# VectorE empties the up bank right behind the norm, and o's low part is made between q's and k's

## The chip, the cores and the metric

The kernel runs on one core of one Trainium2 chip. The metric is the device time of one execution in microseconds (us). Before the change three runs gave 794.05, 796.18 and 797.39 us; the median is 796.18. One more execution was recorded by the hardware profiler; it took 795.6 us, and its span, on which all positions below are counted, is 793.8 us.

## The reference, cut to what matters

```python
x = L0_attn_x                                    # 1 x 4096 x 256, float32
x = x + attention(layernorm(x), w_qkv, w_out)    # 16 heads of 16, rope, phi = elu(.) + 1,
                                                 # causal linear attention: running sums of k*v and of k
x = x + experts(layernorm(x), Wg, Wu, Wd, Wr)    # 8 experts, 256 wide, all of them computed:
                                                 # h = silu(x @ Wg) * (x @ Wu); sum over experts of w * (h @ Wd)
return x
```

The routing weights `w` come from `sigmoid(x @ Wr / temperature)` with a zone test and a top-2 fallback. All is float32; the kernel reaches that precision by splitting each operand into a high and a low part and adding three products.

## The kernel before, in words

The 4096 tokens are cut into 32 tiles of 128 for attention, and into 8 blocks of 512 (four tiles) for the experts. A block has 16 units, two halves of each of eight experts. For one unit TensorE makes `gate(n)` and `up(n)` (six matmuls of 512 columns each), and `down(n)` (twelve of 256 columns). The order of work on each of the five engines is written out by hand; between engines there are semaphores. Each engine goes through its own list strictly in order.

From line 1115 on VectorE's list is a loop over steps `s = 8 to 35`. A step works on three things at once: tile `a = s` (its q, k, v), tile `c = s - 1` (its attention output, projection and second layernorm) and four units `n` to `n + 3` of the block that lies behind. Every fourth step the routing of one block is done as well (`route_...`, some thirty small VectorE operations); it is called a routing step below. Tiles 7 to 31 are `c` in the 25 steps 8 to 32; in six of these (9, 13, ..., 29) there is routing.

The operations that the change and the prediction touch, with their lines:

- `norm(c)`, line 895: VectorE divides the attention output by its denominator and writes `nat`. TensorE then transposes it (`o_T`, line 387).
- `h_up(n + 1)`, line 1064: VectorE multiplies the gate's silu in `work` by the up product in the PSUM bank `up`, which empties that bank. TensorE's next `up(n + 2)` waits for it, and so does ScalarE's `h_hi(n + 1)`, behind which GpSimd makes `h_lo(n + 1)`.
- `q_lo(a)` and `k_lo(a)`, lines 833 and 851: VectorE makes the low parts of q and k. Both wait for ScalarE's `q_hi` and `k_hi`. SyncE then issues the DMA transposes of q and then of k (lines 1284 and 1291), and TensorE's `scores(a)` wait for both.
- `o_lo(c)`, line 905: VectorE makes the low part of the transposed output, behind ScalarE's `o_hi(c)` (line 627). TensorE's projection `proj(c)` (line 390) waits for it.
- `x1_add(c)`, line 911: VectorE adds the projection to x.

In a step TensorE's list (line 499) is `gate(n)`, `up(n)`, `qkv(a)`, `gate(n + 1)`, `state(c)`, `av(c)`, `down(n - 2)`, `up(n + 1)`, `down(n - 1)`, `o_T(c)`, `gate(n + 2)`, `proj(c)`, `up(n + 2)`, `gate(n + 3)`, `down(n)`, `scores(a)`, `x2_T(c)`, `down(n + 1)`, `up(n + 3)`. ScalarE's, around the place of the change: `exp(a)`, `silu(n + 1)`, `q_hi(a)`, `k_hi(a)`, `h_hi(n)`, `v1(a)`, `o_hi(c)`, `h_hi(n + 1)`, `silu(n + 2)`.

Of the kernel before, what the change touches and what calls it, by code (L numbers as in the profile page):

```python
# [45 lines left out]
def bcast(ap, axis, n):  # L46

    ap = ap.unsqueeze(axis)
    shape = list(ap.shape)
    shape[axis] = n  # L50
    return ap.broadcast_to(shape)
# [16 lines left out]
def build(nc, x, xT, w_qkv, w_out, Wg, Wu, Wd, Wr, temperature, tab, out):  # L68
# [8 lines left out]
    with ctx:  # L77
# [113 lines left out]
        def routed(b, step):  # L191

            return len(ROUTE) * b + ROUTE.index(step) + 1
# [17 lines left out]
        def qk_bank(g):  # L211

            return U if g < NT and g % 2 else R0
# [25 lines left out]
        def live(g):  # L239
            return 0 <= g < NTL  # L240
# [5 lines left out]
        def live_unit(n):  # L246
            return 0 <= n < UNITS * NB
# [469 lines left out]
        def vector_program(v):  # L717
# [58 lines left out]
            def x_lo(g):  # L776
                if not live(g):
                    return
                w.wait_ge(s_xhi, g + 1)
                v.tensor_tensor(xo[1][:, g % 2, :, :], xr[:, g % 2, :, :], xo[0][:, g % 2, :, :].bitcast(F32),  # L780
                                ALU.subtract).then_inc(s_xlo, 1)

            def bn(g):
                if not live(g):
                    return
                w.wait_ge(s_mv, g)
                w.wait_ge(xa_in[g % 4], 16 * (g // 4 + 1))
                v.bn_stats(bst[:, :], xa[:, g % NXA, :]).then_inc(s_bn, 1)

            def mean_var(g):  # L790
                if not live(g):
                    return
                w.wait_ge(s_ve, g)
                v.memset(idle[:, 0:1], 0.0)
                w.wait_ge(s_bn, g + 1)
                v.bn_aggr(mv[:, :], bst[:, :]).then_inc(s_mv, 1)
# [36 lines left out]
            def q_lo(g):  # L833
                if not live(g):
                    return
                w.wait_ge(s_qhi, g + 1)
                w.wait_ge(s_khi, g + 1)
                v.tensor_tensor(q_st[:, :, 2:4, :], bcast(qk_bank(g)[:, 0:D].rearrange("p (h d) -> p h d", d=HD), 2, 2),
                                q_st[:, :, 0:2, :], ALU.subtract).then_inc(s_qlo, 1)

            def mask(g, r):
                if not live(g):
                    return
                w.wait_ge(s_mask, 1)
                w.wait_ge(s_alo, am_free(g, r))
                w.wait_ge(s_qk, 2 * g + r // 2 + 1)
                v.tensor_tensor(am_place(g, r).rearrange("p (h n) -> p h n", h=4),  # L847
                                score_bank(g, r)[:, :].rearrange("p (h n) -> p h n", h=4), bcast(cmask[:, :], 1, 4),
                                ALU.mult).then_inc(s_amask, 1)

            def k_lo(g):
                if not live(g):
                    return
                k_s = k_st[:, g % 2, :, :, :]
                w.wait_ge(s_qhi, g + 1)
                w.wait_ge(s_khi, g + 1)
                v.tensor_tensor(k_s[:, :, 1::2, :], bcast(qk_bank(g)[:, D:].rearrange("p (h d) -> p h d", d=HD), 2, 2),
                                k_s[:, :, 0::2, :], ALU.subtract).then_inc(s_klo, 1)
# [36 lines left out]
            def norm(g):  # L895
                if not live(g):
                    return
                w.wait_ge(s_colmean, 2)
                w.wait_ge(s_x2T, g)
                w.wait_ge(s_rec, g + 1)  # L900
                v.scalar_tensor_tensor(out=nat[:, :].rearrange("p (h d) -> p h d", d=HD), in0=osb[:, :, 0:HD],
                                       scalar=1.0 / ASCALE, in1=bcast(rec[:, :], 2, HD), op0=ALU.mult,
                                       op1=ALU.mult).then_inc(s_norm, 1)

            def o_lo(g):
                if not live(g):
                    return
                w.wait_ge(s_ohi, g + 1)
                v.tensor_tensor(ox[1][:, :, :], oT, ox[0][:, :, :].bitcast(F32), ALU.subtract).then_inc(s_olo, 1)
# [47 lines left out]
            def route_sum(b):  # L957
                if not 0 <= b < NB:
                    return
                w.wait_ge(s_logit, b + 1)  # L960
                v.tensor_reduce(R["s2"], logits, AX.X, ALU.add).then_inc(s_route, 1)
# [32 lines left out]
            def route_first(b):  # L994
                if not 0 <= b < NB:
                    return
                w.wait_ge(s_route, routed(b, "eq"))
                v.scalar_tensor_tensor(out=R["c"], in0=R["eq"], scalar=99.0, in1=io, op0=ALU.mult,
                                       op1=ALU.add).then_inc(s_route, 1)
                w.wait_ge(s_route, routed(b, "w0"))  # L1000
                v.tensor_reduce(Q["ws"], R["w0"], AX.X, ALU.add).then_inc(s_route, 1)
                w.wait_ge(s_route, routed(b, "c"))
                v.tensor_reduce(Q["ix"], R["c"], AX.X, ALU.min).then_inc(s_route, 1)
                w.wait_ge(s_route, routed(b, "ws"))
                v.tensor_scalar(Q["no"], Q["ws"], 1e-8, None, ALU.is_lt).then_inc(s_route, 1)

            def route_second(b):
                if not 0 <= b < NB:
                    return
                w.wait_ge(s_route, routed(b, "ix"))  # L1010
                v.tensor_tensor(R["s1"], io, bcast(Q["ix"], 2, E), ALU.is_equal).then_inc(s_route, 1)
                w.wait_ge(s_route, routed(b, "s1"))
                v.scalar_tensor_tensor(out=R["nd"], in0=R["s1"], scalar=9.0, in1=R["dist"], op0=ALU.mult,
                                       op1=ALU.add).then_inc(s_route, 1)
                w.wait_ge(s_route, routed(b, "nd"))
                v.tensor_reduce(Q["m2"], R["nd"], AX.X, ALU.min).then_inc(s_route, 1)
                w.wait_ge(s_fb, b + 1)
                v.tensor_tensor(R["fw"], R["fb"], bcast(Q["no"], 2, E), ALU.mult).then_inc(s_route, 1)
# [45 lines left out]
            def h_up(n):  # L1064
                if not live_unit(n):
                    return
                w.wait_ge(s_g, n + 1)
                w.wait_ge(s_up, n + 1)
                v.tensor_tensor(hb[:, n % 2, :], hb[:, n % 2, :], U[:, :], ALU.mult).then_inc(s_h, 1)  # L1069
# [5 lines left out]
            def acc(n, t):  # L1075

                if not live_unit(n):
                    return
                b, e_ = n // UNITS, n % UNITS // KI
                xs = xa[:, (NT * b + t) % NXA, :]  # L1080
                w.wait_ge(*((s_last, t + 1) if n == LAST + 2 else (s_down, n // KI * KI + KI)))
                w.wait_ge(s_route, routed(b, "wo"))
                w.wait_ge(s_x2n, NT * b + t + 1)
                w.wait_ge(s_acc, NT * (n // KI) + t - 3)
                v.scalar_tensor_tensor(out=xs, in0=y_bank(n, t),  # L1085
                                       scalar=wo[:, b % 2, t, e_:e_ + 1], in1=xs, op0=ALU.mult, op1=ALU.add).then_inc(s_acc, 1)
# [28 lines left out]
            for s in range(8, STEPS):  # L1115
                a, c, n = s, s - 1, NT * (s - LAG)
                router = (s - LAG) // NT if (s - LAG) % NT == 0 else -1
                mask(c, 2); acc(n - 4, 0); bn(a + 1); mask(c, 3); route_sum(router)
                mean_var(a + 1); x_lo(a + 1); acc(n - 4, 1); acc(n - 4, 2); acc(n - 4, 3); h_up(n)
                var_eps(a + 1); route_zone(router); route_nearest(router); cos(a); st_add(c); rope(a); o_sum(c, 0)  # L1120
                o_sum(c, 1); den_max(c); phi(a); route_weight(router); den_rec(c); 
                route_first(router); norm(c); route_second(router); q_lo(a); k_lo(a); o_lo(c); h_up(n + 1)
                route_tie(router); x1_add(c); acc(n - 2, 0); bn2(c); route_ix2(router); acc(n - 2, 1)
                mean_var2(c); acc(n - 2, 2); route_s2(router); var_eps2(c); acc(n - 2, 3)
                h_up(n + 2); route_both(router); ln2(c); mask(a, 0); x2_lo(c); mask(a, 1); route_out(router)
                h_up(n + 3)

            n = LAST
# [240 lines left out]
```

## Time and profile before

| | |
|---|---|
| median of three runs | 796.18 us (794.05 to 797.39) |
| the profiled execution, its span | 795.6 us, 793.8 us |
| TensorE matmul busy | 772.2 us, 97% |
| TensorE weight load busy | 668.2 us, 84% |
| VectorE busy | 607.7 us, 77% |
| GpSimd busy | 481.9 us, 61% |
| ScalarE busy | 466.3 us, 59% |
| chain that ended last | TensorE 86%, VectorE 6%, GpSimd, ScalarE, DMA and issue 2% each |

Times of rows are microseconds from the start of the span. A matmul's end in the trace is modelled, and matmuls are pipelined, so the starts are what one compares: from the start of one group to the start of the next is what the group costs. An operation of VectorE or ScalarE also overlaps the next by some 0.1 us.

### The profile page before, as it was taken

The numbers are of one execution on the slowest core, as the hardware profiler recorded it, in microseconds if no ns is written. First come the engines' busy times: TensorE is split into PE (matmuls) and PEld (weight loads), VectorE is DVE, ScalarE is ACT, GpSimd is POOL, SyncE is SP. The second block draws the span as 40 slices with busy tenths as digits, with TensorE's granted clock in tenths as the row PEclk, the third lists the DMA queues.
The fourth block names the chain that finished last, engine by engine and source line by source line (L and its number), as shares of the span: only waits on it lengthen the run. The fifth ranks groups of instructions, "written<-read, shape, count | busy, mean of one in ns | idle before, by whom it ended". The sixth has DMA issues, their size and how long they took to land.

```text
span 793.8 us, 18445 instructions
## 1 busy us (share of the span) xinstructions
PE 772.2 (97%) x6864; PEld 668.2 (84%) x6864; DVE 607.7 (77%) x1565; ACT 466.3 (59%) x886; POOL 481.9 (61%) x537
## 2 busy tenths in 40 slices
PE   9778899999999999999999999999999999999998
PEld 8666788888888888888888888888888888888887
DVE  7898877879777797778877797788877788756343
ACT  5665776656656656565666566657656666634222
POOL 4886667756566576655666656566676655653322
PEclk9999999999999999999999999999999999999999
DMA  6635331122211031222201221120111121100000
GB/s 171 147 81 111 79 68 47 41 43 68 42 40 29 17 68 41 41 44 65 41 15 31 43 67 42 41 43 19 51 42 41 40 54 28 28 2 27 1 1 26
DMA packets 97320, 38.28 MB, mean 48 GB/s; under 512 B 74192, under 2 KB 96976, under 8 KB 97232
## 3 DMA queue, kind: packets, MB, share of 16 engines
q1 hardware_dynamic: 90704, 30.83, 18.0%
q10 hardware_dynamic: 6528, 6.29, 2.7%
q8 instruction: 54, 0.88, 0.5%
q14 instruction: 34, 0.28, 0.1%
HBM read 16.13 MB, written 4.19 MB: 26 GB/s over the span
## 4 chain that ended last, share of the span: by engine, by line
PE 86%; DVE 6%; POOL 2%; ACT 2%; DMA 2%; issue 2%; SPq 0%; ACTq 0%; DVEq 0%; POOLq 0%
PE y L478 21%; PE up L444 21%; PE gate L444 21%; PE front L304 5%; PE front L305 3%; PE back L356 3%; PE back L400 2%; PE up L375 2%; PE up L412 1%; PE front L327 1%; DMA qT<-q_st 1%; PE back L344 1%; PE front L425 1%; PE back L327 1%; PE y L275 1%
## 5 line engine op out<-in xcount | busy, mean ns | idle before, releaser
L1230 POOL TENSOR_TENSOR h_lo<-work,h_hi 128x512 fp32r<-128x512 f32 x126 | 163.3, 1296 | 63.8 <-ACT h_hi L683 63.0
L1201 POOL TENSOR_TENSOR a_lo<-am,a_hi 128x512 f16<-128x512 f32 x120 | 142.2, 1186 | 52.1 <-ACT a_hi L610 49.6
L478 PE MATMUL y<-wd_hi,h_hi 128*128 128x256 f32 x504 | 145.9, 289 | 0.0
L478 PE MATMUL y<-wd_lo,h_hi 128*128 128x256 f32 x504 | 140.6, 279 | 0.0
L478 PE MATMUL y<-wd_hi,h_lo 128*128 128x256 f32 x504 | 140.4, 278 | 0.0
L1069 DVE TENSOR_TENSOR work<-work,up 128x512 f32<-128x512 f32 x128 | 86.9, 679 | 62.9 <-PE up L444 62.8
L683 ACT ACTIVATE h_hi<-work 128x512 fp32r<-128x512 f32 x126 | 79.3, 629 | 60.6 <-DVE work L1069 33.7
L1085 DVE SCALAR_TENSOR_TENSOR xa<-y,wo,xa 128x256 f32<-128x256 f32 x252 | 111.5, 470 | 2.0 <-PE y L478 2.0
L610 ACT ACTIVATE a_hi<-am 128x512 f16<-128x512 f32 x120 | 74.7, 625 | 41.9 <-DVE am L847 38.3
L478 PEld LDWEIGHTS y<-wd_hi,h_hi 128*128 128x128 f32 x504 | 94.7, 188 | 4.2 <-issue 0.2
L478 PEld LDWEIGHTS y<-wd_lo,h_hi 128*128 128x128 f32 x504 | 94.9, 188 | 2.7
L478 PEld LDWEIGHTS y<-wd_hi,h_lo 128*128 128x128 f32 x504 | 95.2, 189 | 0.0
L675 ACT ACTIVATE work<-gate 128x512 f32<-128x512 f32 x128 | 75.8, 592 | 32.5 <-PE gate L444 18.7
L444 PE MATMUL gate<-x_hi,wg_hi 128*128 128x512 f32 x256 | 82.6, 404 | 0.4 <-ACT work L675 0.4
L1189 POOL TENSOR_TENSOR vs<-vs,vx 128x256 f32<-128x256 f32 x32 | 21.5, 673 | 98.7 <-ACT vx L597 98.7
L444 PE MATMUL up<-x_hi,wu_hi 128*128 128x512 f32 x256 | 81.0, 398 | 0.1
L444 PE MATMUL gate<-x_lo,wg_hi 128*128 128x512 f32 x256 | 80.1, 394 | 0.0
L444 PE MATMUL gate<-x_hi,wg_lo 128*128 128x512 f32 x256 | 79.9, 394 | 0.0
L444 PE MATMUL up<-x_lo,wu_hi 128*128 128x512 f32 x256 | 79.6, 392 | 0.0
L444 PE MATMUL up<-x_hi,wu_lo 128*128 128x512 f32 x256 | 79.5, 392 | 0.0
L1180 POOL TENSOR_TENSOR rop<-qk,tabs 128x256 f32<-128x256 f32 x64 | 46.1, 738 | 30.9 <-ACT qk L555 30.9
L444 PEld LDWEIGHTS gate<-x_hi,wg_lo 128*128 128x128 f32 x256 | 48.3, 189 | 11.0
(227 smaller groups left out, 1773.8 us busy)
## 6 DMA issues: line engine op xcount, KB each, us to landing
xr<-xT SPq DMA_DIRECT2D x32, 128.0 KB, 2.5
xa<-x SPq DMA_DIRECT2D x32, 128.0 KB, 2.5
out<-xa SPq DMA_DIRECT2D x32, 128.0 KB, 1.7
xa<-Wg ACTq DMA_DIRECT2D x8, 256.0 KB, 2.7
work<-Wd ACTq DMA_DIRECT2D x8, 256.0 KB, 3.3
work<-Wu ACTq DMA_DIRECT2D x8, 256.0 KB, 2.9
work<-w_qkv SPq DMA_DIRECT2D x2, 384.0 KB, 3.6
kT<-k_st SPq DMA_TRANSPOSE x32, 3.1
```

The costliest lines, as they stand in the source:

```text
L304: pe.matmul(qk_bank(g)[:, :], lhs, wqkv_p[wi][:, k, 0:2 * D], start=first, stop=last)
L305: m = pe.matmul(R1[:, 0:D], lhs, wqkv_p[wi][:, k, 2 * D:], start=first, stop=last)
L444: m = pe.matmul(ps, weights[wi][:, e_, k, m_ * P:(m_ + 1) * P], x2[xi][:, b % 2, k, :], start=(n == 0), stop=(n == 3 * KD - 1))
L478: m = pe.matmul(y_bank(n, t), h_at(hi, n)[:, t * P:(t + 1) * P], wd_p[wi][:, u // KI, u % KI, :], start=(n % KI == 0 and (t % 2 == 0 or n ...
L610: act.activation(a_p[0][:, heads(r), :], am_place(g, r).rearrange("p (h n) -> p h n", h=4), ACT.Copy).then_inc(s_ahi, 1)
L675: act.activation(hb[:, n % 2, :], G[:, :], ACT.Silu).then_inc(s_g, 1)
L683: act.activation(h_at(0, n), hb[:, n % 2, :], ACT.Copy).then_inc(s_hhi, 1)
L1069: v.tensor_tensor(hb[:, n % 2, :], hb[:, n % 2, :], U[:, :], ALU.mult).then_inc(s_h, 1)
L1085: v.scalar_tensor_tensor(out=xs, in0=y_bank(n, t), scalar=wo[:, b % 2, t, e_:e_ + 1], in1=xs, op0=ALU.mult, op1=ALU.add).then_inc(s_acc, 1)
L1180: pool.tensor_tensor(r2_h[:, :, half, :], qk_h[:, :, 1 - half, :], bcast(tabs[:, g // NT % 2, g % NT, at:at + HALF], 1, 2 * H), ALU.mult). ...
L1201: pool.tensor_tensor(a_p[1][:, heads(r), :], am_place(g, r).rearrange("p (h n) -> p h n", h=4), a_p[0][:, heads(r), :], ALU.subtract).then ...
L1230: pool.tensor_tensor(h_at(1, n), hb[:, n % 2, :], h_at(0, n).bitcast(F32), ALU.subtract).then_inc(s_hlo, 1)
```

## The change

Two edits in one line of VectorE's loop. `h_up(n + 1)` goes from behind `o_lo(c)` to right behind `norm(c)`, ahead of the routing's `route_second` and of `q_lo(a)`. And `o_lo(c)` changes places with `k_lo(a)`. Nothing is added or taken away, and the lists of the four other engines stay as they are.

```diff
@@ -1119,7 +1119,7 @@
                 o_sum(c, 1); den_max(c); phi(a); route_weight(router); den_rec(c); 
-                route_first(router); norm(c); route_second(router); q_lo(a); k_lo(a); o_lo(c); h_up(n + 1)
+                route_first(router); norm(c); h_up(n + 1); route_second(router); q_lo(a); o_lo(c); k_lo(a)
                 route_tie(router); x1_add(c); acc(n - 2, 0); bn2(c); route_ix2(router); acc(n - 2, 1)
```

VectorE's instructions in a step without routing, before (-) and now (+). L901 is `norm`, L838 `q_lo`, L857 `k_lo`, L909 `o_lo`, L1069 `h_up`, L916 `x1_add`; behind each stand the semaphores that it waits for:

```order
 L901 SCALAR_TENSOR_TENSOR nat<-osb,rec 128x256 [waits rec,x2_T]
-L838 TENSOR_TENSOR q_st<-front,q_st 128x16x32 [waits k_hi,q_hi]
-L857 TENSOR_TENSOR k_st<-front,k_st 128x32x16
-L909 TENSOR_TENSOR ox_lo<-back,ox_hi 128x256 [waits o_hi]
-L1069 TENSOR_TENSOR work<-work,up 128x512 [waits up,g]
+L1069 TENSOR_TENSOR work<-work,up 128x512 [waits up,g]
+L838 TENSOR_TENSOR q_st<-front,q_st 128x16x32 [waits k_hi,q_hi]
+L909 TENSOR_TENSOR ox_lo<-back,ox_hi 128x256 [waits o_hi]
+L857 TENSOR_TENSOR k_st<-front,k_st 128x32x16
 L916 TENSOR_TENSOR xa<-back,xa 128x256 [waits proj]
```

`h_up` moved up past three operations, and `o_lo` past one; `x1_add` has the same four in front of it.

The same in a routing step, where L1011 to L1018 are the four operations of `route_second` (one of them, L1016, stands between the two pieces of the difference):

```order
 L901 SCALAR_TENSOR_TENSOR nat<-osb,rec 128x256 [waits rec,x2_T]
+L1069 TENSOR_TENSOR work<-work,up 128x512 [waits up,g]
 L1011 TENSOR_TENSOR router<-iota,q_ix 128x32 [waits router_step]
 L1013 SCALAR_TENSOR_TENSOR router<-router 128x32 [waits router_step]
...
 L1018 TENSOR_TENSOR router<-router,q_no 128x32 [waits fb]
 L838 TENSOR_TENSOR q_st<-front,q_st 128x16x32 [waits k_hi,q_hi]
-L857 TENSOR_TENSOR k_st<-front,k_st 128x32x16
-L909 TENSOR_TENSOR ox_lo<-back,ox_hi 128x256 [waits o_hi]
-L1069 TENSOR_TENSOR work<-work,up 128x512 [waits up,g]
+L909 TENSOR_TENSOR ox_lo<-back,ox_hi 128x256 [waits o_hi]
+L857 TENSOR_TENSOR k_st<-front,k_st 128x32x16
```

Here `h_up` also moved past `route_second`.

## Rows read from the trace of the kernel before

**Rows 1.** The page, part 1: busy time, share of the span, instructions.

```profile
PE 772.2 (97%) x6864; PEld 668.2 (84%) x6864; DVE 607.7 (77%) x1565; ACT 466.3 (59%) x886; POOL 481.9 (61%) x537
```

**Rows 2.** 400 to 500 us: busy PE, PEld, DVE, ACT, POOL (instructions); granted clock; DMA share, GB/s.

```profile
400.00:500.00 100.00, 100.00 (x891) 86.25 (x890) 80.23 (x207) 62.48 (x119) 64.61 (x72) 1.00 0.17 39
```

**Rows 3.** Waits, 200 to 700 us: total, times, longest.

```profile
PEld back L400 <- DVE ox_lo L909: 4.8, 22, 0.2
PE front L327 <- DMA kT<-k_st: 0.6, 1, 0.6
```

**Rows 4.** Timeline of TensorE's matmuls, step without routing: start, duration.

```profile
412.03 0.62 PE L444 MATMUL up<-x_lo,wu_hi 128*128 128x512 f32 x2
...
415.03 0.62 PE L444 MATMUL gate<-x_lo,wg_hi 128*128 128x512 f32 x2
415.50 0.47 PE L400 MATMUL back<-wout_hi,ox_hi 128*128 128x256 f32 x2
416.27 0.62 PE L444 MATMUL up<-x_hi,wu_hi 128*128 128x512 f32 x2
```

**Rows 5.** The same in a routing step.

```profile
278.55 0.62 PE L444 MATMUL gate<-x_lo,wg_hi 128*128 128x512 f32 x2
279.01 0.40 PE L400 MATMUL back<-wout_hi,ox_hi 128*128 128x256 f32 x2
279.71 0.62 PE L444 MATMUL up<-x_hi,wu_hi 128*128 128x512 f32 x2
```

**Rows 6.** Timeline of TensorE's weight loads, step without routing, then with.

```profile
415.46 0.30 PEld L400 LDWEIGHTS back<-wout_hi,ox_hi 128*128 128x128 f32 x2 [0.23 <-DVE ox_lo L909]
...
278.91 0.30 PEld L400 LDWEIGHTS back<-wout_hi,ox_hi 128*128 128x128 f32 x2 [0.17 <-DVE ox_lo L909]
```

**Rows 7.** Timeline of VectorE, step without routing.

```profile
412.12 0.42 DVE L901 SCALAR_TENSOR_TENSOR nat<-osb,rec 128x256 f32<-128x256 f32 x1
413.78 0.69 DVE L838 TENSOR_TENSOR q_st<-front,q_st 128x512 f16<-128x512 f32 x1 [1.24 <-ACT k_st L586]
414.39 0.68 DVE L857 TENSOR_TENSOR k_st<-front,k_st 128x512 f16<-128x512 f32 x1
414.99 0.41 DVE L909 TENSOR_TENSOR ox_lo<-back,ox_hi 128x256 fp32r<-128x256 f32 x1
415.32 0.67 DVE L1069 TENSOR_TENSOR work<-work,up 128x512 f32<-128x512 f32 x1
```

**Rows 8.** Timeline of ScalarE, the same step.

```profile
412.11 0.60 ACT L675 ACTIVATE work<-gate 128x512 f32<-128x512 f32 x1
413.08 0.60 ACT L586 ACTIVATE k_st<-front 128x512 f16<-128x512 f32 x1
414.39 0.39 ACT L632 ACTIVATE ox_hi<-back 128x256 fp32r<-128x256 f32 x1
```

**Rows 9.** Timeline of VectorE and ScalarE, routing step.

```profile
275.91 0.42 DVE L901 SCALAR_TENSOR_TENSOR nat<-osb,rec 128x256 f32<-128x256 f32 x1
277.23 0.69 DVE L838 TENSOR_TENSOR q_st<-front,q_st 128x512 f16<-128x512 f32 x1 [0.25 <-ACT k_st L586]
278.44 0.41 DVE L909 TENSOR_TENSOR ox_lo<-back,ox_hi 128x256 fp32r<-128x256 f32 x1
...
277.87 0.39 ACT L632 ACTIVATE ox_hi<-back 128x256 fp32r<-128x256 f32 x1
```

**Rows 10.** Timeline of SyncE's queue: the transposes of q and k.

```profile
414.50 1.24 SPq L1289 DMA_TRANSPOSE qT<-q_st  x1
415.84 1.27 SPq L1296 DMA_TRANSPOSE kT<-k_st  x1
...
279.28 1.28 SPq L1296 DMA_TRANSPOSE kT<-k_st  x1
```

**Rows 11.** The tile kT, 180 to 740 us: how long its transposes take to land.

```profile
DMA to landing us min/median/max: 3.1/3.1/5.3
```

**Rows 12.** Timeline of TensorE: the scores of the step of [rows 4].

```profile
420.53 0.40 PE L327 MATMUL front<-qT,kT 64*128 64x128 f16 x8
```

## The prediction

> **What bounds the kernel now.** I read the page first: TensorE's matmuls are busy 97% of the span, VectorE 77% [rows 1]. Then the table of busy time by stretch: between 400 and 500 us TensorE is busy for the whole 100.00 us at a granted clock of 1.00 (the 2.4 GHz level), VectorE for 80.23 [rows 2]. So in the loop only what TensorE waits for costs anything. The table of waits from 200 to 700 us shows what that is: the weight load of the projection (line 400) waited for `o_lo` in all 22 steps, 4.8 us together, and the scores waited once for k's transpose, 0.6 us [rows 3]. A waiting weight load isn't yet a lost matmul, so I went to the timeline. In a step without routing the projection starts at 415.50 and `up` behind it at 416.27: 0.77 us for six matmuls [rows 4]. In a routing step the same six take 279.01 to 279.71, 0.70 [rows 5]. The gate in front of both paces the same: its last pair starts 0.47 and 0.46 before the projection. The loss is 0.07, and its cause shows in the weight loads: 415.46 in the one, after 0.23 of waiting, 278.91 in the other, after 0.17 [rows 6]. Seen from the start of the gate's last pair that is 0.43 behind and 0.36 behind. A load 0.36 behind costs nothing that I can see; one 0.43 behind costs 0.07, since the second matmul's load is then late too.
>
> The 25 steps of tiles 7 to 31 hold six routing steps, and in the last one no `q_lo` stands ahead of `o_lo`. That leaves 18 steps with this pattern (I read 0.75 to 0.79 in them). All that VectorE's order can give back here is 18 x 0.07 = 1.3 us. Every other distance from group to group repeats to some 0.05 us (but for two or three late DMAs) whether VectorE is early or late, so I take it as TensorE's own pace.
>
> **The change part by part.** Nothing is added, so the sum is of what moves.
>
> `h_up` behind the norm, step without routing. The norm starts at 412.12 and the next operation, `q_lo`, at 413.78, with 1.24 idle in front, waiting for `k_hi` [rows 7]. `h_up` needs the silu, which ends at 412.11 + 0.60 = 412.71 [rows 8], and `up(n + 1)`, whose last pair of matmuls runs from 412.03 to 412.65 [rows 4]. A wait released by ScalarE takes 0.10 here (`k_hi` ends 413.08 + 0.60 = 413.68, `q_lo` starts 413.78), so `h_up` runs 412.81 to 413.48 with the 0.67 of its row [rows 7]. It fits into the idle time with 0.3 to spare, and `q_lo` stays at 413.78. Cost: nothing. If that cover went, every 0.1 by which `h_up` starts after 413.1 would be 0.1 on `q_lo`.
>
> `o_lo` ahead of `k_lo`. `o_lo` needs `o_hi`, which ends at 414.39 + 0.39 = 414.78 [rows 8]; it stands behind `q_lo`, whose successor started 0.61 after it, at 414.39. The later of the two decides: 414.78 + 0.10 = 414.88, against 414.99 now [rows 7]. So `o_lo` comes 0.11 earlier, not the 0.60 of the operation that it passes. The projection's weight load then starts at 415.46 - 0.11 = 415.35, which is 0.32 behind the gate's last pair, ahead of the 0.36 of the routing step that costs nothing. Gain: the whole 0.07, in 18 steps, -1.3 us. Bounds: 0 (the load remains late) and -1.4 (18 x 0.08, with the start of the projection itself).
>
> `k_lo` last of the three. It starts 0.33 behind `o_lo` (the distance from `o_lo` to its successor, 415.32 - 414.99 [rows 7]): 415.21, end 415.89, against 415.07 now. But SyncE isn't ready for it sooner: the transpose of q holds the queue from 414.50 to 415.74 and that of k is issued at 415.84 [rows 10]. So k's transpose goes from 415.84 to about 415.93, 0.09 later. It lands 3.1 later [rows 11], near 419.0, and the scores start at 420.53 [rows 12], 1.5 later. Cost: nothing. The loads of x behind it on the queue move by the same 0.09, for tiles two and more steps ahead. `x1_add`, next on VectorE, needs the projection, which ends near 416.3 (`up` starts behind it at 416.27 [rows 4]); `k_lo` has ended by then.
>
> The routing step has less room. `q_lo` starts 0.25 after the wait for `k_hi` began, at 277.23 [rows 9]. `h_up` now stands in front of `route_second`, and takes 0.60 from start to start as `k_lo` does (414.39 to 414.99 [rows 7]), so `q_lo` moves by 0.60 - 0.25 = 0.35, to 277.58, and lets its successor in at 278.19. `o_hi` ends at 277.87 + 0.39 = 278.26, so `o_lo` starts at 278.36, against 278.44 [rows 9]: no loss, 0.08 to the good, 0.17 between its two conditions. `k_lo` follows at 278.69 and ends at 279.37. SyncE gets q's transpose 0.35 later and k's at 279.28 + 0.35 = 279.63 [rows 10]; it lands near 282.7. The scores come some 5 us behind the projection (415.50 to 420.53 in [rows 4, 12]), so near 284.0: 1.3 of room. Cost of six such steps: 0; bounds 0 and, if `q_lo` held `o_lo` up by the full 0.35, 6 x 0.35 = +2.1.
>
> What `h_up` feeds. The bank `up` is free 2.5 us sooner, but the table of waits has no row of `up` waiting for it: `up(n + 2)` follows the projection at once. `h_hi(n + 1)` can follow `o_hi` at once, and `h_lo(n + 1)` comes some tenths sooner; its reader, `down(n + 1)`, runs behind the scores, after 420.53 [rows 12]. Gain: 0, since TensorE's list has other work there. Bounds 0 and -0.5.
>
> Sum: -1.3 + 0 + 0 = -1.3 us. Against the profiled execution, whose time is 795.6 (span 793.8 and 1.8 around it), that is 794.3. That execution lies 0.6 below the median of 796.18, so for the median I predict 796.2 - 1.3 = 794.9.
>
> **A rule against this sum.** Rows 2 show TensorE's matmuls at 100.00 of 100 us and the weight loads at 86.25. The Trainium skill (Perfetto Trace Analysis, Identifying the Most-Contended Engine) says that matmul busy time is a poor measure of how near TensorE is to its limit, and that the busy share of LDWEIGHTS is a good one. By that rule 13.75% of the loop would be room, and an earlier `h_up` could win more than my rows let me count. It is the last rival below.
>
> **The rivals.**
>
> 1. The wait is only handed on. `o_lo` is released by `o_hi`, 0.11 earlier than now; if the true release is nearer 0.2 than 0.10, the weight load stays late and nothing moves. For it: the gain hangs on 0.11 us. Against: the routing step shows how little is needed. Time: 796.2.
>
> 2. Slower: k's transpose becomes what the scores wait for. It goes out 0.09 later in ordinary steps and 0.35 later in routing steps. Once it took 5.3 us to land instead of 3.1 [rows 11], and TensorE then stood for 0.6 [rows 3]. If its new place, or the loads of x beside it, made that the rule, each of 25 steps would lose 5.3 - 3.1 - 1.5 + 0.1 = 0.8, so +20 us: 815 (with the 1.3 won, still over 814). It decides once landing takes more than 4.5. Against: TensorE waited for it once in the 22 steps of [rows 3], and it is a shift of 0.09 on a queue that is otherwise the same.
>
> 3. Slower by little: in routing steps `q_lo` holds `o_lo` up. It starts to cost when `q_lo` is over 0.17 later than I think. Price 0.35 x 6 = +2.1, less 1.3: 797.0.
>
> 4. TensorE has room. If the pace of the matmuls hid waits for VectorE, then freeing the bank 2.5 us sooner would give back up to the 0.67 of `h_up` in each of 25 steps: 17 us, 779. Against it: the same groups take the same time in routing steps, where VectorE works later, and in the others; a hidden wait would differ.
>
> **How the numbers follow.** Forecast 0.64, rival 1 0.20, rival 3 0.07, rival 2 0.04, rival 4 0.03, and 0.02 for what I haven't seen. The likeliest time is 794.9. The runs of before spread from 794.05 to 797.39 around their median, so a median carries some 1 to 1.5 us of its own; with the forecast (-1.4 to -1.2) and rivals 1 and 3 (0 to +0.8) the range is 793.0 to 797.4, and rivals 2 and 4 are left out of it. A measurement of this kernel can't tell less than about 0.5% (4 us) from no change. Forecast and rivals 1 and 3 all lie inside that, 0.91 together. Faster by more than that: rival 4 and a share of the unseen, 0.04. Slower: rival 2 and the rest, 0.05.
>
> **What would show it.** In the changed kernel's profile: `h_up` starting within 0.2 of the silu's end, and the idle time before `q_lo` down from 1.24 to about 0.6 or less in ordinary steps, and none in routing steps; `o_lo` 0.1 earlier against the norm; the projection's six matmuls at 0.70 in all steps, and the wait of its weight loads down from 4.8 us to about 2.5; `k_lo`'s end just at the moment its transpose is issued; the scores with no new wait for a DMA. The forecast is wrong if the projection still takes 0.77, if the scores or `o_T` show waits in most steps, or if a step without routing gets shorter by more than 0.1 us.

## The result, and the profile after

The changed kernel takes 800.77 us (median of 6 runs, 799.44 to 801.62) against 795.66 for the one before (6 runs): a ratio of 1.0061, 95% interval 1.0045 to 1.0078. It is slower by 5.1 us, where I had forecast 1.3 faster, a median between 793.0 and 797.4, and given "slower" one chance in twenty.

The ordinary steps (those without routing) did what was predicted; the routing steps lost over four times as much as these won. The timeline of TensorE shows both: the first matmul of `qkv` (L304) marks a step. Before the change, a routing step and then an ordinary one:

```profile
267.74 0.40 PE L304 MATMUL front<-wqkv_hi,xo_hi 128*128 128x512 f32 x1
...
290.31 0.39 PE L304 MATMUL front<-wqkv_hi,xo_hi 128*128 128x512 f32 x1
...
312.84 0.39 PE L304 MATMUL front<-wqkv_hi,xo_hi 128*128 128x512 f32 x1
```

After it, the same two:

```profile
269.39 0.40 PE L304 MATMUL front<-wqkv_hi,xo_hi 128*128 128x512 f32 x1
...
292.99 0.39 PE L304 MATMUL front<-wqkv_hi,xo_hi 128*128 128x512 f32 x1
...
315.43 0.39 PE L304 MATMUL front<-wqkv_hi,xo_hi 128*128 128x512 f32 x1
```

The routing step went from 22.57 to 23.60 us, +1.03; the ordinary one from 22.53 to 22.44, -0.09. The other steps repeat this within some hundredths, but for a few with a late DMA in either kernel, so 6 x 1.03 - 18 x 0.08 = +4.7 of the 5.1 us.

The ordinary step, VectorE's timeline after, answers to [rows 7]:

```profile
416.18 0.69 DVE L1069 TENSOR_TENSOR work<-work,up 128x512 f32<-128x512 f32 x1 [0.22 <-ACT work L675]
417.20 0.69 DVE L838 TENSOR_TENSOR q_st<-front,q_st 128x512 f16<-128x512 f32 x1 [0.33 <-ACT k_st L586]
418.22 0.42 DVE L909 TENSOR_TENSOR ox_lo<-back,ox_hi 128x256 fp32r<-128x256 f32 x1 [0.33 <-ACT ox_hi L632]
418.56 0.68 DVE L857 TENSOR_TENSOR k_st<-front,k_st 128x512 f16<-128x512 f32 x1
419.80 0.42 DVE L916 TENSOR_TENSOR xa<-back,xa 128x256 f32<-128x256 f32 x1 [0.56 <-PE back L400]
```

The norm started at 415.53. `q_lo` starts 1.67 behind it, as before (1.66), `o_lo` 2.69 behind instead of 2.87, and the projection's six matmuls take 0.69 to 0.72 us in every step. The row of `PEld back L400` waiting for `ox_lo` [rows 3] is gone from the table of waits. In its place stand three new rows on `down` (L478), from 200 to 700 us ("issue" is time in which the engine waited for nothing that the profile shows):

```profile
PEld y L478 <- issue: 3.7, 5, 0.7
PE y L478 <- DVE xa L1085: 2.8, 10, 0.3
PEld y L478 <- DVE xa L1085: 2.1, 5, 0.4
```

Five and ten times: once and twice in each routing step of the stretch. TensorE's timeline in one of them shows the price. The last pair of the gate starts at 283.64 and `down` 0.96 later, where it was 0.45 before, and halfway through `down` another 0.39 goes (the matmuls of 256 columns otherwise start 0.11 to 0.12 apart). That is 0.9 of the 1.03. After:

```profile
283.64 0.62 PE L444 MATMUL gate<-x_lo,wg_hi 128*128 128x512 f32 x2
284.60 0.36 PE L478 MATMUL y<-wd_hi,h_hi 128*128 128x256 f32 x1 [0.34 <-DVE xa L1085]
...
285.26 0.28 PE L478 MATMUL y<-wd_hi,h_lo 128*128 128x256 f32 x1
285.76 0.38 PE L478 MATMUL y<-wd_hi,h_hi 128*128 128x256 f32 x1 [0.22 <-DVE xa L1085]
```

Before:

```profile
282.00 0.62 PE L444 MATMUL gate<-x_lo,wg_hi 128*128 128x512 f32 x2
282.45 0.28 PE L478 MATMUL y<-wd_hi,h_hi 128*128 128x256 f32 x1
```

`down(n)` writes PSUM (the memory that matmuls write to) where VectorE's four `acc(n - 2, .)` (L1085) must first have read out the earlier `down`; each adds its part to `xa`, weighted. They stand behind `x1_add` in VectorE's list. Why they are late is in VectorE's own rows. After:

```profile
280.88 0.78 DVE L1024 TENSOR_TENSOR router<-router,q_m 128x32 f32<-128x32 f32 x1
281.70 1.22 DVE L1026 SCALAR_TENSOR_TENSOR router<-router,iota 128x32 f32<-128x32 f32 x1
282.84 0.41 DVE L916 TENSOR_TENSOR xa<-back,xa 128x256 f32<-128x256 f32 x1
```

Before:

```profile
279.37 0.65 DVE L1024 TENSOR_TENSOR router<-router,q_m 128x32 f32<-128x32 f32 x1
280.05 0.19 DVE L1026 SCALAR_TENSOR_TENSOR router<-router,iota 128x32 f32<-128x32 f32 x1
280.16 0.42 DVE L916 TENSOR_TENSOR xa<-back,xa 128x256 f32<-128x256 f32 x1
```

L1024 and L1026 are `route_tie`; both read two inputs in SBUF, the on-chip memory that the engines share. L1026 is the same instruction on 128x32 elements, and took 1.22 us instead of 0.19. Counted from the norm (277.57 and 275.91), it starts at 4.13 and 4.14, but `x1_add` behind it starts at 5.27 instead of 4.25: 1.02 later, and so does each `acc`, within 0.01. GpSimd's timeline says what else was going on. After:

```profile
280.33 2.54 POOL L1230 TENSOR_TENSOR h_lo<-work,h_hi 128x512 fp32r<-128x512 f32 x2
```

Before:

```profile
278.67 1.29 POOL L1230 TENSOR_TENSOR h_lo<-work,h_hi 128x512 fp32r<-128x512 f32 x1
280.32 1.29 POOL L1230 TENSOR_TENSOR h_lo<-work,h_hi 128x512 fp32r<-128x512 f32 x1 [0.35 <-ACT h_hi L683]
```

Before, GpSimd stood still for 0.35 us between `h_lo(n)` and `h_lo(n + 1)`, waiting for `h_hi(n + 1)`, and L1026 ran in just that gap (280.05 to 280.24). Since `h_up(n + 1)` is early, `h_hi(n + 1)` is early, and the two `h_lo` run back to back until 282.87; L1026 ends at 282.92. My theory (the port theory below) was that VectorE and GpSimd share a way into SBUF, so that VectorE's operation can't read beside GpSimd's and waits inside its own busy time. In ordinary steps the two `h_lo` now run back to back too (418.64, 2.55 us), but no operation with both inputs in SBUF stands there. The rivals were that VectorE's order by itself, or one of its own semaphores, makes the step late.

### The profile page after: what moved, and what is told of

Its sections match the earlier page's. It is cut to its first block, busy times and chain, and to the rows that moved or that the text cites. A ratio compares the mean times of both kernels' runs of the same rounds, so it can differ in the third digit from the quotient of the medians.

```text
span 799.5 us, 18445 instructions
## 1 busy us (share of the span) xinstructions
PE 771.5 (96%) x6864; PEld 667.7 (84%) x6864; DVE 618.4 (77%) x1565; ACT 466.0 (58%) x886; POOL 480.4 (60%) x537
## 4 chain that ended last, share of the span: by engine, by line
PE 76%; DVE 10%; ACT 5%; issue 4%; DMA 2%; POOL 2%; SPq 0%; ACTq 0%; DVEq 0%; POOLq 0%
PE up L444 19%; PE gate L444 19%; PE y L478 18%; PE front L304 5%; PE front L305 3%; PE up L375 2%; PE back L356 2%; PE back L400 2%; DVE xa L1085 1%; PE up L412 1%; DMA qT<-q_st 1%; PE front L327 1%; DMA kT<-k_st 1%; ACT L675 1%; DVE k_st L857 1%
## 5 line engine op out<-in xcount | busy, mean ns | idle before, releaser
L478 PE MATMUL y<-wd_hi,h_hi 128*128 128x256 f32 x504 | 146.9, 291 | 3.4 <-DVE xa L1085 3.4
L478 PE MATMUL y<-wd_lo,h_hi 128*128 128x256 f32 x504 | 140.6, 279 | 0.0
L478 PE MATMUL y<-wd_hi,h_lo 128*128 128x256 f32 x504 | 140.4, 279 | 0.0
L1069 DVE TENSOR_TENSOR work<-work,up 128x512 f32<-128x512 f32 x128 | 87.2, 682 | 67.0 <-PE up L444 63.2
L1085 DVE SCALAR_TENSOR_TENSOR xa<-y,wo,xa 128x256 f32<-128x256 f32 x252 | 111.5, 470 | 2.0 <-PE y L478 2.0
L478 PEld LDWEIGHTS y<-wd_hi,h_hi 128*128 128x128 f32 x504 | 94.7, 188 | 10.9 <-issue 4.4
L478 PEld LDWEIGHTS y<-wd_lo,h_hi 128*128 128x128 f32 x504 | 94.9, 188 | 2.4
L478 PEld LDWEIGHTS y<-wd_hi,h_lo 128*128 128x128 f32 x504 | 95.2, 189 | 0.0
```

The source lines that it names most:

```text
L478: m = pe.matmul(y_bank(n, t), h_at(hi, n)[:, t * P:(t + 1) * P], wd_p[wi][:, u // KI, u % KI, :], start=(n % KI == 0 and (t % 2 == 0 or n ...
L1085: v.scalar_tensor_tensor(out=xs, in0=y_bank(n, t), scalar=wo[:, b % 2, t, e_:e_ + 1], in1=xs, op0=ALU.mult, op1=ALU.add).then_inc(s_acc, 1)
```

## The experiments

Each is an edit of the changed kernel; the differences are shortened to the calls that matter. Each ratio is against runs of the kernel before on the same chip.

**The second edit alone.**

```diff
-norm(c); h_up(n + 1); route_second(router); q_lo(a); o_lo(c); k_lo(a)
+norm(c); route_second(router); q_lo(a); o_lo(c); k_lo(a); h_up(n + 1)
```

> The second edit alone: o_lo ahead of k_lo, h_up back behind them in all steps. Theory (port): VectorE's route_tie operations have both inputs in SBUF, and GpSimd's h_lo holds them up while it runs; in the changed kernel h_lo(n+1) follows h_lo(n) without the gap of 0.35 us that was there before, and L1026 takes 1.22 instead of 0.19. With h_up back, that gap returns in routing steps and L1026 takes 0.19 again, so nothing is lost there. But in ordinary steps h_up now ends about 0.5 us later than before (o_lo waits for o_hi with VectorE idle, then k_lo, then h_up), up(n+2) waits some 0.4 for it, 18 steps: 795.7 - 1.3 + 7 = about 802, all of the loss in ordinary steps. Rival (order): the routing step is late because o_lo, k_lo stand otherwise, whatever GpSimd does; then the routing steps stay 1.05 longer here.

Measured: 803.14, ratio 1.0100 (1.0083 to 1.0117). The size was right, and so was its place in the ordinary steps: `up` waits for `h_up`, in the waits from 200 to 700 us

```profile
PEld up L444 <- DVE work L1069: 7.1, 22, 0.3
```

L1026 takes 0.19, and a routing step 22.88 us, not the 23.6 that the rival (the order of `o_lo` and `k_lo` by itself) asks for. I had missed that routing steps also lose some 0.3, since `h_up` is late there too. So the two edits belong together: `o_lo` waits for `o_hi`, and without `h_up` ahead of it VectorE idles and then makes `h_up` late.

**The first edit alone.**

```diff
-route_second(router); q_lo(a); o_lo(c); k_lo(a)
+route_second(router); q_lo(a); k_lo(a); o_lo(c)
```

> The first edit alone: h_up right behind the norm, o_lo behind k_lo as before. Port theory: the collision is there as in the changed kernel (L1026 1.2 us, six routing steps 1.05 longer: +6.3), and the 0.07 in 18 ordinary steps is not won: 795.7 + 6.3 = 802.0, or 1.3 slower than the changed kernel. Rival (the swap is at fault): no loss in routing steps, 795.7.

Measured: 801.79, ratio 1.0081 (1.0067 to 1.0096). As the port theory said. Groups of VectorE, 200 to 700 us (count, busy, mean ns, idle before):

```profile
L1026 DVE SCALAR_TENSOR_TENSOR router<-router,iota 128x32 f32<-128x32 f32 x5 | 6.1, 1222 | 0.2
L1024 DVE TENSOR_TENSOR router<-router,q_m 128x32 f32<-128x32 f32 x5 | 4.8, 959 | 0.0
```

Routing steps take 23.60 us as in the changed kernel, ordinary ones 22.53 as before. The loss comes with `h_up`'s move, not with the swap.

**`route_tie` later, in routing steps.**

```diff
-route_tie(router); x1_add(c); acc(n - 2, 0); bn2(c); route_ix2(router); acc(n - 2, 1)
-mean_var2(c); acc(n - 2, 2); route_s2(router); var_eps2(c); acc(n - 2, 3)
+x1_add(c); acc(n - 2, 0); bn2(c); acc(n - 2, 1); route_tie(router)
+mean_var2(c); acc(n - 2, 2); route_ix2(router); var_eps2(c); acc(n - 2, 3); route_s2(router)
```

> The changed kernel with route_tie moved behind acc(n-2, 1), and route_ix2 and route_s2 each one place on, in routing steps; ordinary steps are unchanged. Port theory: VectorE's two-input operations no longer stand in front of x1_add while GpSimd runs h_lo(n) and h_lo(n+1); x1_add starts 4.0 to 4.3 us behind the norm instead of 5.28, down(n) waits little: 794.4, at most 796. Rival (VectorE has simply too much to do in a routing step since the change): the same work is only reordered ahead of acc(n-2, 3), and down(n) still waits about 1 us in its second half: 800.

Measured: 794.53, ratio 0.999 (0.998 to 1.000), with the two `h_lo` still back to back (278.27, 2.55 us). The same operations, now behind them, take

```profile
280.94 0.18 DVE L1024 TENSOR_TENSOR router<-router,q_m 128x32 f32<-128x32 f32 x1
281.15 0.19 DVE L1026 SCALAR_TENSOR_TENSOR router<-router,iota 128x32 f32<-128x32 f32 x1
```

The rival of too much work on VectorE falls: all of it is still in front of `acc(n - 2, 3)` but for `route_s2`, and the loss is gone.

**`h_up` behind `k_lo` in routing steps only.**

```diff
+if router < 0: h_up(n + 1)
 route_second(router); q_lo(a); o_lo(c); k_lo(a)
+if router >= 0: h_up(n + 1)
```

> The changed kernel in ordinary steps, but in the six routing steps h_up stands behind k_lo again (o_lo stays ahead of k_lo). Port theory: ordinary steps 0.07 to 0.08 shorter than before, routing steps as before, L1026 0.19: 795.7 - 1.3 = 794.4. If the loss were not in the routing steps' h_up: 800.

Measured: 796.38, ratio 1.001 (1.0001 to 1.0019). L1026 is back at 0.19, but this missed 794.4 by 2. The waits name it: `up` waits for `h_up` in the five routing steps of the stretch.

```profile
PEld up L444 <- DVE work L1069: 1.5, 5, 0.3
```

From start to start the projection and `up` are 0.37 us longer there (3.83 instead of 3.46 up to `down`), the whole step 0.33; 6 x 0.33 = 2.0, as in the first experiment.

**L1026 with one input.** Its `scalar_tensor_tensor` becomes `tensor_scalar(R["c"], R["eq"], 99.0, None, mult)`, which leaves out the addition of the expert's index.

> The changed kernel with the second operation of route_tie (L1026) as a tensor_scalar with one input in SBUF instead of a scalar_tensor_tensor with two; it leaves out the addition of the expert's index. Same place, same 128x32 output, same wait on router_step. Port theory: it runs beside GpSimd's h_lo(n+1) in about 0.19 us instead of 1.22, x1_add in routing steps starts 1.0 earlier, time 794.4 to 795. Rival (the operation waits for something of its own engine, as the slow operation in front of it or its semaphore): still 1.2 us, 800.8.

Measured: 800.11, ratio 1.0057 (1.0042 to 1.0072). A miss:

```profile
L1026 DVE TENSOR_SCALAR router<-router 128x32 f32<-128x32 f32 x5 | 6.1, 1211 | 0.2
```

So either the number of inputs isn't what matters, or the theory is wrong. The pairs that follow tell which.

**A pair of operations in the ordinary steps**, of three kinds, where `route_tie` would stand; the second of each waits for the first:

```diff
+tensor_tensor(pair[:, 0, :], cmask[:, 0:32], cmask[:, 32:64], add)   # first kernel: two inputs
+tensor_tensor(pair[:, 1, :], pair[:, 0, :], cmask[:, 32:64], add)
+tensor_scalar(pair[:, 0, :], cmask[:, 0:32], 99.0, None, mult)       # second: tensor_scalar
+tensor_scalar(pair[:, 1, :], pair[:, 0, :], 99.0, None, mult)
+tensor_reduce(pair[:, 0, :], cmask[:, 0:64], X, add)                 # third: tensor_reduce
+tensor_reduce(pair[:, 1, 0:16], pair[:, 0, :], X, add)
```

> The changed kernel with two small operations added where route_tie would stand in the ordinary steps (18 of them): 128x32, both inputs in SBUF, the second waiting for the first. Port theory: the first lasts until h_lo(n) ends (about 0.8 us), the second until h_lo(n+1) ends (about 1.2), x1_add starts 1.3 later, and TensorE loses 0.5 to 1.0 in each of 18 steps: 810 to 819. Rival (only the length of the work counts): two operations of 0.19 in a place where VectorE idles 0.5 cost nothing: 800.8.

> The control to the one before: the same two added operations, same place, size and waits, but each a tensor_scalar with one input in SBUF. Port theory: 0.2 us each and no cost, 800.8 as the changed kernel. If a tensor_scalar from SBUF to SBUF is held up too, they take 0.8 and 1.2 like the others. Rival (added semaphores or instructions cost by themselves): as slow as the two-input pair.

> Second control to the two pairs: the same place and waits in 18 ordinary steps of the changed kernel, but two tensor_reduce operations from SBUF to SBUF (128x32 from 128x64, 128x16 from 128x32). Theory (a shared read path that only some kinds of operation take): tensor_reduce and bn_stats were not held up beside h_lo in the traces so far (L1033 0.17 us, L923 0.42), so they take 0.2 us each and cost little: 800.8 to 802. Rival (any VectorE operation that reads only SBUF is held up beside GpSimd, or the added instructions and semaphores cost by themselves): 0.8 and 1.2 us and 812, like the others.

Measured: 813.66 (1.0223, 1.0206 to 1.0240), 811.94 (1.0207, 1.0192 to 1.0222) and 800.03 (1.0053, 1.0040 to 1.0066). The tile of the pair in the three (min/median/max in ns):

```profile
L1071 DVE TENSOR_TENSOR pair<-cmask x18: 812/817/819, 165.5 to 709.0; 128x32 f32<-128x32 f32 x18
L1073 DVE TENSOR_TENSOR pair<-pair,cmask x18: 1222/1228/1230, 166.4 to 709.9; 128x32 f32<-128x32 f32 x18
```

```profile
L1071 DVE TENSOR_SCALAR pair<-cmask x18: 803/805/815, 163.2 to 706.5; 128x32 f32<-128x32 f32 x18
L1073 DVE TENSOR_SCALAR pair<-pair x18: 1219/1226/1229, 164.1 to 707.4; 128x32 f32<-128x32 f32 x18
```

```profile
L1071 DVE TENSOR_REDUCE pair<-cmask x18: 208/210/213, 164.2 to 695.8; 128x32 f32<-128x64 f32 x18
L1073 DVE TENSOR_REDUCE pair<-pair x18: 186/186/188, 164.5 to 696.0; 128x16 f32<-128x32 f32 x18
```

The same place, the same waits, the same added semaphore: a `tensor_reduce` costs 0.2 us and nothing in time, a `tensor_tensor` or a `tensor_scalar` between SBUF and SBUF costs 0.8 and 1.2 us and 11 to 13 us in all. The rivals (own semaphores, added instructions, mere length) fall, and so does my narrower form of the theory, that it takes two inputs: the `tensor_scalar` pair reads one input each. The second of the pair ends with GpSimd: with `tensor_tensor`, at 427.72 where the second `h_lo` ends at 427.68.

**Routing steps wholly as before**, ordinary ones as changed.

```diff
+if router < 0: h_up(n + 1); q_lo(a); o_lo(c); k_lo(a)
+else: route_second(router); q_lo(a); k_lo(a); o_lo(c); h_up(n + 1)
```

> Ordinary steps as in the changed kernel, routing steps wholly as before (q_lo, k_lo, o_lo, h_up). The kernel that kept o_lo ahead of k_lo in routing steps had its h_up 0.45 later than before, and up(n+2) waited 0.37 for it, six times. Expected: 795.7 - 18 x 0.07 = 794.4, with L1026 at 0.19 and routing steps at 22.56. If it stays at 796.4, the 0.37 is not what that kernel lost.

Measured: 793.36, ratio 0.9968 (0.9957 to 0.998): faster than both kernels. In its profile routing steps take 22.55 to 22.58 (but two of the five between 200 and 700 us 22.69 and 22.75) and ordinary ones 22.45, so the order accounts for about 1.4 of the 2.6 us. The profile of before also has one step 0.7 longer for a late transpose, which this one hasn't; whether their other runs differ in that isn't known, and the remaining half microsecond stays open.

**`route_tie` ahead of `q_lo` in routing steps.**

```diff
+else: route_second(router); route_tie(router); q_lo(a); o_lo(c); h_up(n + 1); k_lo(a)
```

> Routing steps: route_second, then route_tie, then q_lo, o_lo, h_up, k_lo; ordinary steps as in the changed kernel. route_tie runs before GpSimd starts (v_rest about 2.1 us behind the norm), so it should take 0.18 and 0.19; q_lo comes about 0.15 later than before, h_up ends about 0.1 earlier than before, x1_add follows the projection at once. Port theory: 794.4 or a few tenths less. Rival (route_tie's cost is its own, wherever it stands): it takes 1 to 2 us and q_lo is late: 800 or more.

Measured: 793.94, ratio 0.998 (0.9967 to 0.9993). With GpSimd not yet at work both operations are short:

```profile
275.82 0.19 DVE L1024 TENSOR_TENSOR router<-router,q_m 128x32 f32<-128x32 f32 x1
276.05 0.19 DVE L1026 SCALAR_TENSOR_TENSOR router<-router,iota 128x32 f32<-128x32 f32 x1
```

This order and that of the last experiment can't be told apart: 0.9967 to 0.9993 and 0.9957 to 0.998 overlap.

**Only GpSimd's order changed**, in routing steps; VectorE's list is that of the changed kernel.

```diff
-h_lo(n + 1); rstd2_pow(c); st_rest(c)
+st_rest(c); h_lo(n + 1); rstd2_pow(c)
```

> VectorE's list is that of the changed kernel, unchanged; only GpSimd's is different, in routing steps: st_rest(c) stands ahead of h_lo(n+1), which holds h_lo(n+1) back by some 1.3 us. Port theory: L1026 runs in the gap, 0.19 us, x1_add starts 4.3 behind the norm instead of 5.28; a later two-input operation (L1039) may be held up by some 0.5 instead: 794.4 to 796.5. Rival (the fault lies within VectorE's order): 800.8.

Measured: 796.42, ratio 1.0008 (0.9999 to 1.0017): over 4 of the 5 us come back without a touch on VectorE's list.

```profile
279.18 0.19 DVE L1026 SCALAR_TENSOR_TENSOR router<-router,iota 128x32 f32<-128x32 f32 x1
279.29 0.42 DVE L916 TENSOR_TENSOR xa<-back,xa 128x256 f32<-128x256 f32 x1
```

`h_lo(n)` ended at 279.10 and `h_lo(n + 1)` began at 280.48. The routing steps still take 22.93 us, 0.36 more than before, because the later `h_lo(n + 1)` now holds up another operation with two inputs in SBUF, as was expected above; it stands ahead of the last `acc`, which starts 6.99 behind the norm instead of 6.64. Groups of VectorE, 200 to 700 us (0.18 us each in the kernel before):

```profile
L1039 DVE TENSOR_TENSOR router<-iota,q_ix 128x32 f32<-128x32 f32 x5 | 2.7, 534 | 0.0
```

This is the test I rely on most, with the three pairs.

## Why the prediction was wrong

**The ordinary steps: right.** `h_up` fitted into the idle time, `q_lo` didn't move, the projection went from 0.77 to 0.70 us. `o_lo` came 0.18 earlier instead of 0.11. 18 steps won some 0.08 each, as the term of -1.3 said.

**k's transpose: right.** It went out 0.02 later against the norm and the scores had no new wait.

**The routing steps: the step that failed is "What h_up feeds".** It says that `h_lo(n + 1)` comes some tenths sooner and that this gains 0, "since TensorE's list has other work there". In a routing step that closes GpSimd's gap, L1026 lasts 1.22 us instead of 0.19, and `x1_add`, the `acc` and `down(n)` are late behind it: a term of 6 x 1.03 = +6.2 us that the sum doesn't have. I followed `h_lo` to its reader and stopped; I never asked what runs beside it. Its bounds, 0 and -0.5, should have held +1.0 in each of six steps. The paragraph on the routing step was right as far as it went: its estimate for `k_lo`'s end, 3.46 behind the norm, came out at 3.39, and `o_lo` held nothing up. It ended with `k_lo`. The next instruction on VectorE, `route_tie`, wasn't in the sum, since it had not moved against its neighbours.

**The trace before had the sign.** L1024 took 0.65 us for 128x32 elements, where L1013, of the same size, took 0.19; it had been held up by the end of `h_lo(n)` (278.67 + 1.29 = 279.96, L1024's end 280.02). A plainer sign stood in the groups of VectorE from 200 to 700 us (busy us, mean ns). Both operations subtract 128x256 elements. The first has both inputs in SBUF, and from 140 to 760 us it starts beside GpSimd's `a_lo` in 23 of 24 cases, and takes 0.41 us in the one other; the second has one input in PSUM:

```profile
L780 DVE TENSOR_TENSOR xo_lo<-xr,xo_hi 128x256 fp32r<-128x256 f32 x20 | 21.7, 1083 | 0.0
L954 DVE TENSOR_TENSOR x_lo<-up,x_hi 128x256 fp32r<-128x256 f32 x22 | 9.3, 425 | 5.9 <-ACT x_hi L640 5.9
```

An operation with a busy time far above that of its likes was the row to ask about.

**The rivals.** Rival 1 (the wait is only handed on) fell: the weight load of the projection no longer waits. Rival 3 had the right place (routing steps) and the wrong mechanism; rival 2 (the transpose) left no sign, with one wait of the scores as before. Nor did rival 4 (hidden room in TensorE): the best of all orders tried gains 0.3%, with the weight loads busy 86.21 of 100 us after the change too. That is also evidence against reading the 13.75% as room in this kernel.

**A rule that would have told me.** The runs show VectorE's `tensor_tensor`, `scalar_tensor_tensor` and `tensor_scalar` between SBUF and SBUF held up until GpSimd's `tensor_tensor` ends, `tensor_reduce` not, and `x1_add` (one input in PSUM, 0.42 us at 419.80, inside the two `h_lo`) not. The Trainium skill (SBUF — State Buffer, Who interferes with whom) says the same: a VectorE operation with two inputs in SBUF contends with a GpSimd one that reads SBUF, `tensor_scalar` can do so in its two-port modes, `tensor_reduce` never does, and the loser waits for the whole instruction. These runs agree: 1.22 us for two inputs and for `tensor_scalar`, 0.21 and 0.19 for `tensor_reduce`, and, for operations of 128x32, an end 0.04 to 0.07 behind GpSimd's. That the `tensor_scalar` here ran in such a mode no run shows, nor that a port is what the two engines share; those are that page's reasons, not mine.

## What to carry to other kernels

An operation that comes sooner starts others sooner on engines that share something with it. When a move fills an idle gap on one engine, ask who was using that gap: here 0.35 us of GpSimd waiting was the only time, between the start of the one `h_lo` and the end of the other, in which L1026 could run in 0.19 us. And follow the engine's list past the last instruction moved, up to the next one that TensorE waits for.

## What the hardware showed that I had not expected

- A VectorE operation of 0.19 us takes 1.22 us beside a GpSimd `tensor_tensor` of 1.27 (L1026 in the changed kernel, 1.33 in its last routing), and the profile books it as busy, not as a wait: the table of waits has no row for L1026.
- VectorE gets its turn between two GpSimd operations that run back to back (L1024 ended at 281.66, some 0.06 after the first `h_lo`, taken as half of the pair), but not inside one. GpSimd's pair took 2.54 us together, no longer than twice 1.29, so it lost nothing that shows to the 128x32 operation.
- It depends on the kind of operation and not on its size alone: `tensor_scalar` with one input is held up like one with two, `tensor_reduce` of the same size isn't.
